# Loading layer 1's first data from layer 0, and a shorter hand-over from projections to gate products, in a two-layer transformer kernel

## The reference

```python
xn = _layernorm(x, axis=-1)
s = _L0_attn_ref(xn, ...)        # per token, over the head dimension: 16 x 16 scores
g = _silu(_L0_ffn_ref(xn, ...))  # 2 of 3 experts, chosen by the first token of a batch
x = x + s * g
xn = _layernorm(x, axis=-1)
s = _L1_attn_ref(xn, Wq, Wk, Wv, Wo)   # causal, 32 query and 8 key heads of 16, rotary embedding
g = _silu(_L1_ffn_ref(xn, ...))        # silu(gate) * up, then down; weights packed in 4 bits with scales and zeros
x = x + s * g
```

## Time and profile before

| | us |
|---|---|
| median of 3 runs | 1476.67 |
| lowest and highest | 1471.11, 1478.86 |
| the profiled execution's own time | 1469.95 |
| its span | 1468.2 |
| TensorE busy | 1337.5 (91%) |
| VectorE busy | 1058.9 (72%) |
| ScalarE busy | 618.0 (42%) |
| GpSimd busy | 334.9 (23%) |
| granted TensorE clock, mean over the span | 0.95 |

### The profile page before, as it was taken

One profiled execution on the slowest core, in us unless ns is written; L12 is line 12 of the kernel. 1 busy time (PEld: TensorE's weight loads), 2 busy tenths in 40 slices (PEclk: granted clock), 3 DMA queues, 4 the chain that ended last, 5 costly groups with the idle time before them and its releaser, 6 DMA issues.

```text
span 1468.2 us, 19974 instructions
## 1 busy us (share of the span) xinstructions
PE 1337.5 (91%) x6642; PEld 924.9 (63%) x6642; DVE 1058.9 (72%) x2495; ACT 618.0 (42%) x859; POOL 334.9 (23%) x387
## 2 busy tenths in 40 slices
PE   3788988992998899999999998999999999999998
PEld 2557676772765677777777764555555555555467
DVE  6887978684787555555555476888888888888557
ACT  4633755452442111111111111666666666666662
POOL 2653667361332000000000000222112222212221
PEclk9978998995999899999999995999999999999999
DMA  6101200005344100000000050111122132231002
GB/s 213 63 24 63 72 16 29 0 29 184 96 124 135 53 27 27 25 22 22 22 13 12 5 97 0 34 34 34 34 44 56 34 90 62 63 68 29 2 29 86
DMA packets 45165, 76.11 MB, mean 52 GB/s; under 512 B 9556, under 2 KB 16804, under 8 KB 45076
## 3 DMA queue, kind: packets, MB, share of 16 engines
q1 hardware_dynamic: 43086, 73.36, 18.1%
q10 hardware_dynamic: 1990, 1.62, 0.4%
HBM read 55.67 MB, written 19.01 MB: 51 GB/s over the span
## 4 chain that ended last, share of the span: by engine, by line
PE 63%; DVE 6%; ACT 2%; issue 2%; DVEq 1%; ACTq 1%; DMA 0%; POOL 0%; SPq 0%; POOLq 0%
PE d_bank L1835 12%; PE d_bank L37 10%; PE d_bank L1875 10%; PE d_bank L1859 9%; PE d_bank L39 9%; PE d_bank L38 9%; PE d_bank L1883 1%; DVE mx_first L1595 1%; DVEq L1598 1%; DVE hl L1451 1%; DVE d_bank L1592 1%; PE d_bank L1704 1%; DVE hs L1448 1%; PE d_bank L1814 1%; ACT hh L1350 1%
## 5 line engine op out<-in xcount | busy, mean ns | idle before, releaser
L1386 ACT ACTIVATE prob<-d_bank 128x1024 f32<-128x1024 f32 (+3 forms) x384 | 302.3, 811 | 212.8 <-PE d_bank L1859 209.2
L1592 DVE CUSTOM_DVE_ANT_0 d_bank<-d_bank,mask 128x128 f32<-128x128 f32 (+3 forms) x512 | 246.2, 504 | 43.4 <-PE d_bank L1835 35.8
L1835 PE MATMUL d_bank<-kst,qst 96*128 96x512 f32 (+3 forms) x768 | 264.4, 386 | 5.4 <-DVE mx_first L1595 3.2
L1835 PEld LDWEIGHTS d_bank<-kst,qst 96*128 96x128 f32 x768 | 145.4, 194 | 145.1 <-DVE mx L1592 51.7
L1859 PE MATMUL d_bank<-qst,kst 98*128 98x512 f32 (+3 forms) x768 | 210.7, 357 | 0.5 <-ACT prob L1386 0.5
L1251 POOL TENSOR_SCALAR_AFFINE_SELECT prob<-prob 128x256 f32<-128x256 f32 x256 | 103.9, 406 | 449.9 <-ACT prob L1386 448.4
L1595 DVE TENSOR_REDUCE mx_first<-d_bank 128x1 f32<-128x512 f32 x256 | 176.3, 689 | 27.0 <-PE d_bank L1835 19.7
L1875 PE MATMUL d_bank<-prob,vst 128*32 128x512 f32 (+3 forms) x1536 | 164.5, 500 | 1.1 <-POOL prob L1251 1.1
L1342 ACT ACTIVATE hs<-d_bank 128x512 f32<-128x512 f32 (+1 forms) x44 | 26.3, 598 | 304.1 <-PE d_bank L39 304.1
L37 PE MATMUL d_bank<-xtl,wgh 128*128 (+1 forms) x352 | 141.3, 402 | 11.0 <-DVE v_all L1537 11.0
L1859 PEld LDWEIGHTS d_bank<-qst,kst 98*128 98x128 f32 x768 | 130.0, 192 | 19.0 <-ACT prob L1386 8.2
(11 more groups left out here) (256 smaller groups left out, 2419.1 us busy)
## 6 DMA issues: line engine op xcount, KB each, us to landing
wst<-L_ffn_w SPq DMA_DIRECT2D x8, 1024.0 KB, 6.9
qst<-q_scr SPq DMA_DIRECT2D x32, 256.0 KB, 4.8
qw<-L_ffn_qweight_gu SPq DMA_DIRECT2D x40, 128.0 KB, 2.6
xb<-L_attn_x SPq DMA_DIRECT2D x4, 1024.0 KB, 6.7
x_d<-xb SPq DMA_DIRECT2D x4, 1024.0 KB, 4.3
xb<-x_d SPq DMA_DIRECT2D x4, 1024.0 KB, 6.7
q_scr<-qh SPq DMA_DIRECT2D x16, 256.0 KB
q_scr<-ql SPq DMA_DIRECT2D x16, 256.0 KB
```

Of the source, the lines that this page charges most:

```text
L1386: act.activation(prob[:, c // 2 % 2, c % 2 * 2:c % 2 * 2 + 2, lo:], score_bank[c % 2][:, :, lo:], ACT.Exp, scale=D ** -0.5).then_inc(exp_d ...
L1592: dve.tensor_tensor_reduce(sc, sc, mask[:, CH - w:CH], 1.0, LEAST, ALU.add, ALU.max, mx[:, u, h % 2, h // 2, q:q + 1]).then_inc(spare_free, 1)
L1835: pe.matmul(spare_bank(number)[:, 0:w], qst[u][0:M_ROW, h // 2, q * P:q * P + P], kst[u][0:M_ROW, h % 2, at:at + w], start=True, stop=True ...
```

## The change

1. Layer 0 and layer 1 share `ident`, the first x1 buffer, `wqkv` and three semaphores. After the store of x1's chunk 2, and once the experts' weights are split, SyncE in layer 0 loads x1's chunk 0 and Wq, Wk, Wv. All of layer 0's arrays get fixed places, so that these buffers lie on `wst`; three x buffers become separate arrays.
2. Layer 0 no longer waits for the landing of its last store. Layer 1 waits for it on SyncE ahead of the reload of the x buffer.
3. All loads at the start of layer 1 are issued by SyncE, `mask` and `fixed` later. ScalarE issues none.
4. The six weight blocks are turned into six banks without a wait, and ScalarE makes their high parts before it normalizes.
5. The sixth piece is loaded after (3, 0), spread after tile 3 and made after (3, 2).
6. The last values are turned into bank 2, without a wait for ropes. TensorE doesn't wait for ropes and values ahead of the gate loop; the second gate tile (`h_ready`) and the first down product (`acc_ready`) wait for the values instead.
7. `hh` and `hl` move, and the waits for `q_free` are spread: 18 ahead of the loop on ScalarE, 19 at the second tile, 20 on VectorE ahead of `hl`.

```diff
@@ layer0, sync
             for c in range(CHUNKS):
                 u = c % UB
                 sp.wait_ge(x1_ready, (c + 1) * TPC)
-                sp.dma_start(x1v[:, c], xb[:, u]).then_inc(xout[u], 16)
+                sp.dma_start(x1v[:, c], xb[u][:, :, :]).then_inc(xout[u], 16)
...
-            sp.wait_ge(xout[0], 32)
+                if c == 2:
+                    sp.wait_ge(w1_ready, SL * B)
+                    sp.dma_start(shared.xb[:, 0], x1v[:, 0]).then_inc(shared.x_in, 16)
+                    sp.wait_ge(w2_ready, SL * B)
+                    Wq1, Wk1, Wv1 = next_qkv
+                    sp.dma_start(shared.wqkv[:, 0:KT], Wq1.rearrange("(o p) e -> p o e", p=P)).then_inc(shared.w_in, 16)
+                    sp.dma_start(shared.wqkv[:, KT], Wk1).then_inc(shared.w_in, 16)
+                    sp.dma_start(shared.wqkv[:, KT + 1], Wv1).then_inc(shared.w_in, 16)
             sp.wait_ge(xout[1], 16)
             sp.wait_ge(xout[2], 16)
@@ layer1
-        hh, hl = place("hh", [P, 2, CH], F32R, 193), place("hl", [P, 2, CH], F32R, 197)
+        hh, hl = place(nc, "hh", [P, 2, CH], F32R, 199), place(nc, "hl", [P, 2, CH], F32R, 189)
...
-        MADE = {(1, 2): 0, (2, 0): 1, (2, 2): 2, (3, 0): 3, (3, 1): 4, (3, 3): 5}
-        ROWS = {(1, 2): 0, (2, 1): 1, (2, 3): 2, (3, 1): 3, (3, 2): 4, (3, 4): 5}
-        LOADS = {(1, 3): (2,), (2, 3): (3, 4), (3, 1): (5,)}
+        MADE = {(1, 2): 0, (2, 0): 1, (2, 2): 2, (3, 0): 3, (3, 1): 4, (3, 2): 5}
+        ROWS = {(1, 2): 0, (2, 1): 1, (2, 3): 2, (3, 1): 3, (3, 2): 4, (3, 3): 5}
+        LOADS = {(1, 3): (2,), (2, 3): (3, 4), (3, 0): (5,)}
...
         def value_bank(c):
-            return bank[:, 0 if c < CHUNKS - 1 else 4]
+            return bank[:, 0 if c < CHUNKS - 1 else 2]
@@ layer1, sync
-            sp.dma_start(xb[:, 0], x1v[:, 0]).then_inc(xin[0], 16)
-            sp.dma_start(wqkv[:, 0:KT], Wq.rearrange("(o p) e -> p o e", p=P)).then_inc(w_in, 16)
-            sp.dma_start(wqkv[:, KT], Wk).then_inc(w_in, 16)
-            sp.dma_start(wqkv[:, KT + 1], Wv).then_inc(w_in, 16)
             sp.dma_start(xb[:, 1], x1v[:, 1]).then_inc(xin[1], 16)
+            sp.dma_start(rotate[:, :], rotate_d).then_inc(rotate_in, 16)
+            sp.dma_start(cos[:, :], cos_d).then_inc(table_in, 16)
+            sp.dma_start(sin[:, :], sin_d).then_inc(table_in, 16)
+            small = lambda to, a: sp.dma_start(to, a).then_inc(s_in, 16)
...
             quants(0, 0, *PIECES[0])
             quants(0, 0, *PIECES[1])
+            sp.wait_ge(shared.x1_stored, 32)
             reload(2)
             keep_small_arrays()
+            sp.dma_start(mask[:, :], mask_d).then_inc(const_in, 16)
+            sp.dma_start(fixed[:, :, :], fixed_d).then_inc(const_in, 16)
@@ layer1, scalar
-            act.dma_start(ident[:, :], ident_d).then_inc(const_in, 16)
...
-            normalize(0, range(TPC))
             for o in range(OT):
                 act.wait_ge(w_tp, o + 1)
-                act.activation(wth[:, :, o * P:o * P + P], bank[:, 2 + o % 2].rearrange("p (k q) -> p k q", k=KT),
+                act.activation(wth[:, :, o * P:o * P + P], bank[:, 2 + o].rearrange("p (k q) -> p k q", k=KT),
                                ACT.Copy).then_inc(w_hi, 1)
+            normalize(0, range(TPC))
             high_parts(0, range(TPC))
...
-            act.wait_ge(q_free, CHUNKS * ROT)
+            act.wait_ge(q_free, CHUNKS * ROT - 2)
...
+                        if s == 0 and n == 1:
+                            act.wait_ge(q_free, CHUNKS * ROT - 1)
@@ layer1, vector
-            dve.sem_inc(h_ready, 2)
+            dve.sem_inc(h_ready, 1)
             dve.sem_inc(hl_ready, 2)
             dve.sem_inc(w_ready, 1)
-            dve.sem_inc(acc_ready, 1)
...
+                if s == 0:
+                    dve.wait_ge(q_free, CHUNKS * ROT)
                 dve.tensor_tensor(hl[0:rows, v], hs[0:rows, v], hh[0:rows, v].bitcast(F32), ALU.subtract).then_inc(hl_ready, 1)
...
             values(CHUNKS - 1)
+            dve.drain().then_inc(h_ready, 1)
+            dve.sem_inc(acc_ready, 1)
             each_pair(dve, body)
@@ layer1, tensor
             pe.wait_ge(w_in, 48)
-            pe.wait_ge(ident_in, 16)
-            pe.wait_ge(const_in, 48)
             for o in range(OT):
-                if o >= 2:
-                    pe.wait_ge(w_lo, o - 1)
                 for k in range(KT):
-                    mm = pe.transpose(bank[:, 2 + o % 2, k * P:k * P + P], wqkv[:, o, k * P:k * P + P], ident[:, :])
+                    mm = pe.transpose(bank[:, 2 + o, k * P:k * P + P], wqkv[:, o, k * P:k * P + P], ident[:, :])
...
-                if c == CHUNKS - 1:
-                    pe.wait_ge(rope_ready, CHUNKS * ROT + 1)
...
             turn_values(CHUNKS - 1)
-            pe.wait_ge(qf_ready, CHUNKS * OT + 2)
-            pe.wait_ge(rope_ready, CHUNKS * ROT + 2)
-            pe.wait_ge(v_ready, CHUNKS + 1)
             each_pair(pe, body)
```

More of the change, by code:

```diff
@@ L109, in layer0 @@
         x3_in = sem("x3_in")
[L110 removed]
+        xout = [shared.x1_stored] + [sem(f"xout{u}") for u in range(1, UB)]
         w_in = [sem(f"w_in{u}") for u in range(WB)]
@@ L895, in layer1 @@
         IG, IR, IC = E // P, ZR, INTER // ZR
-        xb = place("xb1", [P, 2, TPC, E], F32, 0)
-        cos, sin = place("cos", [P, T], F32, 16), place("sin", [P, T], F32, 20)
-        qf, qc = place("qf", [P, 2, CH], F32, 24), place("qc", [P, 2, CH], F32, 28)
-        wth, wtl = place("wth", [P, KT, QKT], F32R, 147.5), place("wtl", [P, KT, QKT], F32R, 159.5)
-        qh, ql = place("qh", [P, HALVES, CH], F32R, 189), place("ql", [P, HALVES, CH], F32R, 195)
-        rotate = place("rotate", [P, P], F32, 201)
@@ new lines, in layer1 @@
+        cos, sin = place(nc, "cos", [P, T], F32, 16), place(nc, "sin", [P, T], F32, 20)
+        qf, qc = place(nc, "qf", [P, 2, CH], F32, 24), place(nc, "qc", [P, 2, CH], F32, 28)
+        wth, wtl = place(nc, "wth", [P, KT, QKT], F32R, 147.5), place(nc, "wtl", [P, KT, QKT], F32R, 159.5)
+        qh, ql = place(nc, "qh", [P, HALVES, CH], F32R, 189), place(nc, "ql", [P, HALVES, CH], F32R, 195)
+        rotate = place(nc, "rotate", [P, P], F32, 201)
+        stats, mv = place(nc, "stats1", [P, TPC, 6], F32, 201.5), place(nc, "mv1", [P, TPC, 2], F32, 201.625)
@@ new lines, in layer1 @@
+        hh, hl = place(nc, "hh", [P, 2, CH], F32R, 199), place(nc, "hl", [P, 2, CH], F32R, 189)
+        mask = place(nc, "mask", [P, CH], F32, 204)
+        mt = place(nc, "mt", [HG * QB, STACKS, P], F32R, 206)
+        fixed = place(nc, "fixed", [P, 2, 1], F32, 207.5)
+        qst = [place(nc, f"qst{u}", [P, 2, T], F32R, at) for u, at in enumerate((112, 128, 171.5))]
+        kst = [place(nc, f"kst{u}", [P, 2, T], F32R, at) for u, at in enumerate((120, 136, 179.5))]
+        vst = place(nc, "vst", [P, STACKS, QB, 2 * D], F32, 144)
@@ L1268, in _ @@
         def _(act):
-            act.dma_start(ident[:, :], ident_d).then_inc(const_in, 16)
-            act.dma_start(mask[:, :], mask_d).then_inc(const_in, 16)
-            act.dma_start(fixed[:, :, :], fixed_d).then_inc(const_in, 16)
-            act.dma_start(rotate[:, :], rotate_d).then_inc(ident_in, 16)
-            sp_in = lambda out, a: act.dma_start(out, a).then_inc(s_in, 16)
-            flat_gu = lambda a, n: a.rearrange("g f -> (g f)").rearrange("(p c) -> p c", p=n)
-            sp_in(sg[:, :], flat_gu(sc_gu, P))
-            sp_in(zg[:, :], flat_gu(qz_gu, ZR))
-            sp_in(sdn, sc_d)
-            sp_in(zdp[:, :], qz_d)
-            sp_in(shift[:, :], shift_d)
-            sp_in(row[:, :], row_d)
-            sp_in(lane_shift[:, :], lane_shift_d)
-            sp_in(idx[:, 0:IG], gi_gu.rearrange("(p c) -> p c", p=P))
-            sp_in(idx[0:IR, IG:], gi_d.rearrange("(p c) -> p c", p=IR))
             act.sem_inc(qf_ready, 2)
-            act.dma_start(cos[:, :], cos_d).then_inc(table_in, 16)
-            act.dma_start(sin[:, :], sin_d).then_inc(table_in, 16)
             def normalize(c, tiles):
```

187 lines of the change are left out of this document (102 added, 85 removed).

## The result

| | median us | runs |
|---|---|---|
| before | 1473.89 | 4, 1469.97 to 1478.86 |
| changed | 1457.78 | 4, 1452.42 to 1459.84 |
| ratio | 0.9881 | 95% interval 0.9854 to 0.9907 |

The changed kernel is 1.2% faster. The profiled execution took 1452.42, its span is 1450.7 (before 1469.95 and 1468.2).

The account below looks back on a forecast made before the run. TensorE is busy 91% of the span, so only its idle stretches can give time: layer boundary 16.3 plus end of projections 6.1 make 22.4, which off the median 1476.67 gives 1454.3 us; range 1447 to 1463.

Parts of the forecast that it names:

- The boundary's mechanism: Between layers 0 and 1: earlier opening, unbroken transposes and early casts bring the first projection from 371.99 to 355.7, gain 16.3.
- The factors: Start of layer 1: GpSimd's last normalization factor ends at 348.2, hidden behind ScalarE's casts, which end at about 348.6.
- The dropped wait: End of layer 0: 3.9 us of waiting for the last store to land goes away.
- SyncE's queue: Start of layer 1: 13 load issues take 11.0, last landed at 356.5, wanted at 358.5; hidden, 2 us to spare.
- the new short idles: Gate loop's start: three TensorE idles of some 2 us; forecast wrong if the clock falls there and doesn't come back.
- the lower bound: Layer boundary: with all weight transposes slow, the first projection starts at 357.3, gain 14.7.
- The second stretch: From projections to gate products: the last packed load comes 5.19 earlier; gain 6.1, bounds 4.3 to 9.6.
- a third idle: Gate loop's start: TensorE ends products at 484.0, then waits for the next scale rows to about 486.2.
- the block's end waits by itself: Rival, exit of layer 0's block: it drains the store anyway, so 3.9 is lost: 1458.2; chance 0.10.
- the queue: Rival, layer 1's start: SyncE's load issues become the bound; within 0.5% chance 0.06, slower chance 0.04.
- the second gap comes back whole: Rival, ahead of the gate products: another wait ends as late as before, leaving the boundary gain alone: 1460.4; chance 0.09.
- Transposes stay at 1.2 GHz: Rival, weight transposes at layer 1's start: the clock stays low throughout, boundary gives 14.7: 1455.9; chance 0.07.

Follow-up runs that it names:

- run 4: Changed kernel with layer 0's wait for its last store put back: 1456.98 us, ratio to before 0.9893.
- run 5: Changed kernel, but ScalarE normalizes the first chunk ahead of the six weight casts: 1457.58 us, ratio to before 0.9895.
- runs 2: Changed kernel with points 5 to 7 undone (SBUF places stay), so only the layer boundary is changed: 1457.48 us, ratio to before 0.9897.
- Run 3: Kernel before with only points 5 to 7 of the change, the layer boundary as before: 1466.35 us, ratio to before 0.9957.
- run 6: Changed kernel with 34 extra identity transposes on TensorE around the turns of x and ahead of the first projection: 1450.51 us, ratio to before 0.9846.
- run 7: Changed kernel, but SyncE issues the next step's first packed weights ahead of its waits for the last two rope stores: 1452.76 us, ratio to before 0.9874.
- run 1: Changed kernel measured again, unaltered, for a second trace: 1452.49 us, ratio to before 0.9865.
- run 9: Changed kernel unaltered, third time, beside two kernels with filler transposes on one chip: 1456.62 us, ratio to before 0.9869.
- run 12: Changed kernel with 34 filler transposes and early packed weights, plus 30 more fillers in the gate loop's first pass: 1446.4 us, ratio to before 0.9828.

## Why the prediction was right, and where its sizes were off

The forecast was 1454.3 in 1447 to 1463. The three medians of the changed kernel, 1457.78, 1452.49 and 1456.62, lie on both sides of it. They are 16.1, 21.1 and 19.3 below before's on the same chips, 18.8 on the mean, where I had 22.4. That the forecast of the time is nearer than that of the gain is luck: I took the gain off 1476.67, and in the comparison before's median was 1473.89, 2.8 lower.

- **The boundary's mechanism is right, step by step.** Layer 1 opened at 0.91 (forecast 0.9), the transposes took 4.54 (4.9), and the first projection came 14.06 after the store (13.6). The factors, which I had hidden behind the casts, ended at 351.25 while the casts ended at about 351.4, so they were just hidden. The dropped wait was worth 4.1 (run 4) of the 3.9 forecast, the new order 4.1 (run 5). The gain was 15.9 of 16.3.
- **SyncE's queue is no limit.** VectorE made its small arrays at 361.31 right behind its statistics, with no wait for their loads. The 13 issues, 345.47 to 352.66, took 7.2 where I had 11.0.
- **The term that was left out: what TensorE's clock does after the transposes.** I asked whether it would come back, and it did. I did not ask whether it stays, and wrote only of "the new short idles" in the second part. Between the last weight transpose and the first projection TensorE has 16 thin transposes and idles of 1.47, 2.05 and 1.62. Before the change the same turns stood right behind weight transposes, with idles of 1.07 and 1.46, and the first projections ran at full speed. Here the first 11 products ran at 1.2 GHz, 0.2 longer each. This is the 2.3 lost in Q; runs 2 and 3 put it to the boundary, and run 6 takes it away and 1.6 more, which before had lost too. In my sum it was zero, and the lower bound didn't have it either.
- **The second stretch gave 5.6 of 6.1**, inside its bounds of 4.3 to 9.6, and for partly another reason. The packed load came early, the first gate product followed the turn by 0.87 and two short idles stood where forecast (2.48 and 2.32, forecast 2.6 and 2.2). I had the whole end wait for the quants, with a third idle of 1.4 on TensorE. They did come late, but the third idle isn't there: TensorE's own chain, lengthened by eight products at 1.2 GHz, ended at the same time, as run 7 shows. My list of what would make me wrong had the clock fall in the new short idles and not come back. It fell, and it came back after some 3.5 us of products.
- **Layer 0, mostly chance.** The last store's issue lay between 341.44 and 349.51 in the 14 traces. No TensorE instruction of layer 0 is in any of the diffs, though the change gives all of its arrays other places. The two traces with the layer 0 of before have 342.08 and 343.39, the twelve with the changed one 344.7 on the mean, so a cost of a microsecond or two can't be excluded. The row of 318 to 326 of before and of the changed kernel:

```profile
318.00:326.00 8.00, 8.00 (x31) 5.32 (x30) 7.67 (x8) 4.50 (x7) 0.00 (x0) 1.00 0.00 0
```

```profile
318.00:326.00 8.00, 8.00 (x19) 4.58 (x18) 7.58 (x10) 3.50 (x5) 0.17 (x1) 0.57 0.00 0
```

Both are busy throughout; one makes 31 products, the other 19, at a lower clock. Run 3, with the layer 0 of before, also made 19 there, at 0.55. The loads that went into layer 0 don't explain the spread: the changed kernel stored at 342.86 in run 1 and 345.69 in run 9, with the same loads. What makes the clock fall in one execution and not in the next wasn't found.

Of the rivals, *the block's end waits by itself* fell with run 4, *the queue* with the timeline, and *the second gap comes back whole* with G (22.4 against 27.9). *Transposes stay at 1.2 GHz* is half right in its effect: its price, 14.7 instead of 16.3, was not paid, since the windows show 0.86 and 1.00 in 349 to 356; but the low clock came all the same, after the turns. The Trainium skill ("TensorE: Matmul & The Clock Gate", Part 4: PE-mode transpose) says that the clock gate doesn't engage for transposes. The traces here disagree: in the changed kernel the granted clock rose from 0.50 to 1.00 between 346 and 356 with only transposes running, and where transposes alone filled the idles, 34 of them ahead of the projections in run 6 and 30 more in the gate loop in run 12, it stayed at 1.00.

## What to carry to other kernels

Where an edit lets TensorE start earlier behind thin work, put into the sum at which clock the first dense products run, not only when they start. Here, behind sparse transposes with 1.5 to 2 us between them, it had fallen, and 11 products at 0.43 instead of 0.23 cost 2.3 us; transposes that only fill the wait bought that back and more. And when one late operation is advanced without effect, as the quants in run 7, look for a second chain that ended at the same time: from rows 1 to rows 2 each edit alone seemed useless (8.75 and 9.46 after 7.91), and together they gave 6.29. Finally, compare stages from a landmark inside the trace; over 340 us of the same work two executions differed by up to 8 us, four tenths of the effect measured here. Follow them to the end as well: what run 6 had gained in Q its trace lost again in the gate loop.

## What had not been expected of the hardware

- Transposes of the identity, whose result nobody reads, held the granted clock at 1.00 in the idles that they filled. With 34 of them the whole kernel was 4.5 us shorter on the mean of all runs (1450.34 against 1456.62 by the medians on one chip).
- With the fillers Q was 98.44, less than the 100.02 of before. The projections of before had lost 1.6 to the clock as well: eight slow products, with a granted clock of 0.93 in 400 to 410 and 0.90 in 410 to 420, where with the fillers it is 1.00 throughout. TensorE's idle time in Q is 2.7 in both, so no wait shows the loss.
- A wait of 2.3 to 2.7 us behind dense work at 2.4 GHz is sometimes followed by 7 to 13 products at 1.2 GHz, and sometimes not: in the changed kernel's trace the products after the idle of 2.48 stayed 0.23 apart, and of those after the 2.32 eight did not.
